# A decoder layer on one core: rotating the last block's k on GpSimd between the loops, and a last-stage softmax with one exponential

## The reference, cut to what matters

```python
q = (query @ Wq).reshape(nb, q_len, H, D).transpose(0, 2, 1, 3)
k = (key @ Wk).reshape(nb, q_len, KVH, D).transpose(0, 2, 1, 3)
...
q = q * cos + _rotate_half(q) * sin
k = k * cos + _rotate_half(k) * sin
...
scores = jnp.einsum('bhqd,bhkd->bhqk', q, k) / jnp.sqrt(jnp.float32(D))
scores = jnp.where(mask == 0, jnp.float32(-1000000000.0), scores)
attn = jax.nn.softmax(scores, axis=-1)
x = jnp.einsum('bhqk,bhkd->bhqd', attn, v)
return x.transpose(0, 2, 1, 3).reshape(nb, q_len, H * D) @ Wo
```

## Time and profile before

| | |
|---|---|
| median of 3 runs | 2348.61 us (2341.81 to 2349.77) |
| profiled execution | 2350.73 us |
| its span, first to last instruction | 2349.1 us |
| mean granted TensorE clock | 0.95 of full speed |
| busy: TensorE, VectorE | 2086.0 us (89%), 1762.5 us (75%) |
| busy: ScalarE, GpSimd | 1003.9 us (43%), 701.3 us (30%) |

### The profile page before, as it was taken

How to read it: one execution, slowest core, us unless ns; L and a number is a source line. 1 busy time by engine, 2 the same in 40 slices (tenths; PEclk the granted TensorE clock), 3 DMA queues, 4 the chain that set the end, 5 groups by cost and what they waited for, 6 DMA issues and landing times.

```text
span 2349.1 us, 26708 instructions
## 1 busy us (share of the span) xinstructions
PE 2086.0 (89%) x8268; PEld 1192.0 (51%) x8272; DVE 1762.5 (75%) x1735; ACT 1003.9 (43%) x2549; POOL 701.3 (30%) x492
## 2 busy tenths in 40 slices
PE   6877887898999988998999989998999989799988
PEld 2333454345555543445556544345556544477774
DVE  4499994459999996259999996259999994456553
ACT  2544440265555532155545541255545540233331
POOL 0289992401111112401111111501111110456550
PEclk9788999889999999989999999989999999799999
DMA  2579895527888873435888874525887874332210
GB/s 63 165 178 230 210 215 169 146 95 175 176 182 196 184 180 101 154 117 135 186 190 179 186 166 119 186 91 136 190 190 181 188 166 117 103 99 90 86 59 18
DMA packets 117810, 352.12 MB, mean 150 GB/s; under 512 B 14016, under 2 KB 14144, under 8 KB 115296
## 3 DMA queue, kind: packets, MB, share of 16 engines
q0 software_dynamic: 40704, 146.82, 32.3%
q1 hardware_dynamic: 70112, 191.68, 26.6%
q10 hardware_dynamic: 6912, 12.59, 1.4%
HBM read 197.68 MB, written 23.33 MB: 94 GB/s over the span
## 4 chain that ended last, share of the span: by engine, by line
DVE 34%; PE 27%; DMA 17%; issue 14%; ACT 3%; POOL 2%; DVEq 1%; PEldq 1%; SPq 0%; POOLq 0%; PEld 0%; ACTq 0%
DMA xc<-hs 15%; DVE hs L1254 11%; DVE hs L1431 4%; PE acc L1753 4%; PE acc L1631 3%; DVE hs L1261 3%; DVE hs L1245 2%; PE pq L1684 2%; PE acc L1837 2%; PE pq L1714 2%; PE pq L1921 2%; PE pk L1921 2%; PE acc L1766 1%; DVE pzsc L1311 1%; DVE qr L1291 1%
## 5 line engine op out<-in xcount | busy, mean ns | idle before, releaser
L768 POOL DMA_DIRECT2D xc<-hs x192 | 164.1, 860 | 1116.3 <-DVE hs L1261 1095.9
L1254 DVE TENSOR_TENSOR_SCAN hs<-dA,hs 128x1024 f32<-128x1024 f32 x192 | 428.7, 2274 | 0.0
L988 ACT ACTIVATE dA<-dt,aneg 128x504 f32<-128x504 f32 x384 | 253.6, 707 | 320.0 <-DVE hs L1254 319.8
L1684 PE MATMUL pq<-qT,wa 128*128 128x512 f32 x768 | 354.1, 615 | 15.1 <-DVE pzsc L1311 14.9
L1766 PE MATMUL acc<-wb,oT 128*128 128x512 f32 x768 | 352.2, 603 | 3.6 <-ACT oT L976 3.6
L1261 DVE TENSOR_TENSOR hs<-hs,bc 128x1024 f32<-128x1024 f32 x256 | 307.6, 1203 | 2.2
L953 ACT ACTIVATE pr<-pzsc,mx 128x64 f32<-128x64 f32 x512 | 170.8, 335 | 245.1 <-DVE mx L1317 245.1
L1245 DVE TENSOR_TENSOR hs<-u,bc 128x1024 f32<-128x1024 f32 x192 | 227.5, 1217 | 26.6 <-DMA xc<-hs 21.0
L1631 PE MATMUL acc<-xnT,wa 128*128 128x512 f32 x512 | 234.4, 612 | 14.3 <-DMA wa<-in_wx 3.9
L1684 PEld LDWEIGHTS pq<-qT,wa 128*128 128x128 f32 x768 | 146.4, 196 | 189.3 <-issue 177.2
L1766 PEld LDWEIGHTS acc<-wb,oT 128*128 128x128 f32 x768 | 141.2, 193 | 148.0 <-issue 143.9
(11 more groups left out here) (255 smaller groups left out, 3379.2 us busy)
## 6 DMA issues: line engine op xcount, KB each, us to landing
xc<-hs POOLq DMA_DIRECT2D x240, 512.0 KB, 7.0
bc<-bc_rows SPq DMA_DIRECT2D x64, 512.0 KB, 7.5
wa<-in_wq SPq DMA_DIRECT2D x64, 512.0 KB, 10.2
wb<-in_wo SPq DMA_DIRECT2D x64, 512.0 KB, 7.0
wa<-in_wx SPq DMA_DIRECT2D x16, 512.0 KB, 7.0
wa<-in_wz SPq DMA_DIRECT2D x16, 512.0 KB, 3.8
wb<-in_ow SPq DMA_DIRECT2D x16, 512.0 KB, 6.3
wv<-in_wv SPq DMA_DIRECT2D x26, 256.0 KB, 13.1
```

Source lines behind the costliest of these rows:

```text
L768: G.dma_start(xc[:, 2 * c:2 * c + 2, :], hs[:, c, :].rearrange("p (d t) -> p d t", t=T), accum_op=ALU.add).then_inc(s_y[c], 16)
L988: ins = S.activation(to[:, :, 1:SEQ], dt[:, s, :].rearrange("p (b t) -> p b t", t=SEQ)[:, :, 1:SEQ], ACT.Exp, scale=aneg[:, s, bass.ds(jj ...
L1254: V.tensor_tensor_scan(out=hs[:, c, :], data0=dA[:, c % 2, :], data1=hs[:, c, :], initial=0.0, op0=ALU.mult, op1=ALU.add).then_inc(scd.sem, 1)
L1684: ins = M.matmul(pq[:, h, :], wa4(p)[:, k, h * P:(h + 1) * P], qT[:, k, :], start=(k == 0), stop=(k == KE - 1))
```

## The change

Three things. GpSimd rotates the k of block 3 in the gaps after iterations 1 and 2, four heads (two pairs, m = 4 and 5) in each, with the cosines and sines of block 3, which SyncE loads into `oT`. Prefill, VectorE and SyncE wait for the larger counts. The last stage loads turned k straight into `kT`, and the load waits for the scores that read the head before. In the last stage VectorE adds the negated maximum to the scores, ScalarE takes one exponential of 512 columns, VectorE sums it; the high part of o is copied ahead of the exponential, and the low part is made between the sum with the maximum and the sum of the exponentials. The router's small buffers move to `kr` and `k1` for all blocks. The pieces below are in the order of the file: SyncE, GpSimd, ScalarE, VectorE.

```diff
-                            if p == 0 and mamba:
+                            if p == 0:
                                 eng.wait_ge(sd.sem, sd.upto(blk, 1) + jj * 2)
                                 hold(eng)
-                                load_turned_k(blk, jj + 1)
-                            elif p == 0:
-                                eng.wait_ge(krdy.sem, krdy.upto(0, 0) + jj)
-                                hold(eng)
-                                load_raw_k(blk, jj + 1)
+                                load_turned_k(blk, jj + 1, mamba)
...
                     if not nxt:
-                        load_raw_k(i, 0)
+                        eng.wait_ge(sd.sem, sd.upto(blk, PAIRS - 1))
+                        load_turned_k(i, 0, False)
...
+                if attn and nxt:
+                    eng.wait_ge(wod.sem, wod.upto(blk, PAIRS - 1))
+                    hold(eng)
+                    for c in range(2):
+                        eng.dma_start(oT[:, c, :], tscr[NBLK - 1, c]).then_inc(s_cs3, 16)
...
                     for n in range(2):
-                        eng.wait_ge(s_kst[n], i * 32 + 32)
+                        eng.wait_ge(s_kst[n], i * 48 + 32)
...
+                def heads_of(rows, m):
+
+                    if m < pairs:
+                        return rows[i, 2 * m:2 * m + 2]
+                    return rows[NBLK - 1, bass.ds((i - 1) * (KVH // 2) + 2 * (m - pairs), 2)]
...
-                def turn_pair(m):
+                def turn_pair(m, count):
 
                     raw, swp = turning[m % 2]
+                    cos, sin = (cosT[:, :], sinT[:, :]) if m < pairs else (oT[:, 0, :], oT[:, 1, :])
...
-                    if 1 <= m < KVH // 2 - 1:
+                    if 1 <= m < count - 1:
                         load_pair(m + 1)
...
-                    for m in range(KVH // 2):
-                        turn_pair(m)
+                    count = pairs + (2 if attn else 0)
+                    for m in range(count):
+                        if m == pairs:
+                            eng.wait_ge(s_cs3, i * 32)
+                            hold(eng)
+                        turn_pair(m, count)
...
                     if mamba:
-                        eng.wait_ge(s_kst[1], blk * 32 + 32)
+                        eng.wait_ge(s_kst[1], i * 48 - 16)
...
                     eng.wait_ge(smx.sem, smx.upto(blk, o) + jj * 2)
+                    if not mamba:
+                        S.activation(pr[:, :, :], pr[:, :, :], ACT.Exp).then_inc(exd.sem, 1)
+                        return
...
+                    if not mamba:
+                        evac_o(jj, p)
                     if attn and not last:
                         exps(jj, p + 1)
                     if mamba and not last:
                         decay(jj, p + 1, 0)
-                    if attn:
+                    if mamba and attn:
                         evac_o(jj, p)
...
+                def shift_scores(jj, o):
+
+                    eng.wait_ge(lmx.sem, lmx.upto(0, o) + jj * 2)
+                    V.tensor_tensor(pr[:, :, :], sc[:, :, :], mx[:, :].unsqueeze(2).to_broadcast([P, NB, SEQ]),
+                                    ALU.add).then_inc(smx.sem, 1)
+
+                def sum_probs(jj, o):
+
+                    eng.wait_ge(exd.sem, exd.upto(blk, o) + jj * 2)
+                    V.tensor_reduce(sm[:, :], pr[:, :, :], AX.X, ALU.add).then_inc(psm.sem, 1)
...
+                if mamba and attn:
+                    for n in range(2):
+                        eng.wait_ge(s_kst[n], i * 48 - 16)
...
-                    if not mamba and not tail and p == 0:
-                        rope_k(jj + 1)
...
+                    if soft and not mamba:
+                        shift_scores(jj, p + 1)
+                    if not mamba:
+                        o_low(jj, p)
+                    if soft and not mamba:
+                        sum_probs(jj, p + 1)
                     if soft:
                         invert_sum(jj, p + 1)
...
-                    if not mamba:
-                        o_low(jj, p)
```

More of the change, by code:

```diff
@@ L97, in build @@
         vscr = nc.dram_tensor("v_rows", (KVH, P, T), F32, kind="Internal").ap()
-        turned = nc.dram_tensor("k_turned_rows", (NBLK - 1, KVH, P, T), F32, kind="Internal").ap()
+        turned = nc.dram_tensor("k_turned_rows", (NBLK, KVH, P, T), F32, kind="Internal").ap()
         tscr = nc.dram_tensor("rotary_rows", (NBLK, 2, P, T), F32, kind="Internal").ap()
@@ L265, in build @@
         s_cs = sem("rotary_tables_loaded")
+        s_cs3 = sem("last_rotary_tables_loaded")
         s_kraw = [sem(f"raw_k_loaded{n}") for n in range(2)]
@@ L325, in build @@
         s_pid = sem("pos_index_ready")
-        kc1 = stage("pool_k_times_cos", KVH // 2)
-        kc2 = stage("pool_k_times_sin", KVH // 2)
-        kcd = stage("pool_k_turned", KVH // 2)
+        kc1 = stage("pool_k_times_cos", 6)
+        kc2 = stage("pool_k_times_sin", 6)
+        kcd = stage("pool_k_turned", 6)
         otd = stage("tail_o_done", TT)
@@ L334, in build @@
         qt2 = stage("q_times_sin", PAIRS)
-        kt1 = stage("k_times_cos", KVH)
-        kt2 = stage("k_times_sin", KVH)
         qrdy = stage("q_ready", PAIRS)
@@ L339, in build @@
         q2r = stage("q_sin_ready", PAIRS)
-        krdy = stage("k_ready", KVH)
         vrdy = stage("v_ready", KVH)
@@ L360, in build @@
         olo = stage("o_lo_ready", PAIRS)
+        lmx = stage("last_scores_max", PAIRS)
+        psm = stage("last_probs_summed", PAIRS)
         x2r = stage("x2_ready", TT)
@@ L536, in one, with load_turned_k @@
                 z_uses = W_DT if mamba else 0
-                def load_k(b, g, src, to, swapped):
-                    eng.dma_start(to[:, :], src[b, g]).then_inc(s_k1, 16)
-                    for h in range(2):
-                        eng.dma_start(swapped[h * 64:(h + 1) * 64, :], src[b, g, (1 - h) * 64:(2 - h) * 64, :]).then_inc(
+                def load_turned_k(b, g, halves=True):
+                    eng.dma_start(kT[:, :], turned[b, g]).then_inc(s_k1, 16)
+                    for h in range(2 if halves else 0):
+                        eng.dma_start(k2T[h * 64:(h + 1) * 64, :], turned[b, g, (1 - h) * 64:(2 - h) * 64, :]).then_inc(
                             s_kr, 16)
-                def load_raw_k(b, g):
-                    load_k(b, g, kscr, k1, kr)
-                def load_turned_k(b, g):
-                    load_k(b, g, turned, kT, k2T)
                 def load_tables(b):
@@ L837, in one, with turns, slot_use @@
                         rstd(i, ln2, ln2r, TT)
+                pairs = KVH // 2
+                def heads_of(rows, m):
+                    if m < pairs:
+                        return rows[i, 2 * m:2 * m + 2]
+                    return rows[NBLK - 1, bass.ds((i - 1) * (KVH // 2) + 2 * (m - pairs), 2)]
+                def turns(m):
+                    return (i * 6 - 2 if attn else 0) + (m + 1 + LEAD)
+                def slot_use(m):
+                    return (i * 3 - 1 if attn else 0) + m // 2
                 def load_pair(m):
@@ L1316, in max_scores @@
                     eng.wait_ge(srd.sem, srd.upto(blk, o) + jj * 2)
-                    V.tensor_reduce(mx[:, :], sc[:, :, :], AX.X, ALU.max, negate=True).then_inc(smx.sem, 1)
+                    V.tensor_reduce(mx[:, :], sc[:, :, :], AX.X, ALU.max, negate=True).then_inc(
+                        smx.sem if mamba else lmx.sem, 1)
+                def shift_scores(jj, o):
[5 more added lines that the diff above has]
+                    V.tensor_reduce(sm[:, :], pr[:, :, :], AX.X, ALU.add).then_inc(psm.sem, 1)
                 def invert_sum(jj, o):
-                    eng.wait_ge(exd.sem, exd.upto(blk, o) + jj * 2)
+                    if mamba:
+                        eng.wait_ge(exd.sem, exd.upto(blk, o) + jj * 2)
+                    else:
+                        eng.wait_ge(psm.sem, psm.upto(0, o) + jj * 2)
                     V.reciprocal(sm[:, :], sm[:, :]).then_inc(rcp.sem, 1)
@@ L1359, in one @@
                     eng.wait_ge(s_cs, blk * 32 + 32)
+                    rope_q(0, 0)
+                    mask_scores(0, 0)
+                    max_scores(0, 0)
                     if not mamba:
-                        rope_k(0)
-                    rope_q(0, 0)
-                    for part in (mask_scores, max_scores, invert_sum, probs):
-                        part(0, 0)
+                        shift_scores(0, 0)
+                        sum_probs(0, 0)
+                    invert_sum(0, 0)
+                    probs(0, 0)
                     rope_q(0, 1)
```

61 lines of the change are left out of this document (27 added, 34 removed).

## The result

In one comparison on the same chip the kernel before took 2345.58 us (median of 4 runs) and the changed one 2372.56 us (4 runs, 2368.15 to 2379.81): 27.0 us more, a ratio of 1.0118, 95% interval 1.0084 to 1.0151. That is slower, as forecast, and inside the range, but 13 us under the forecast of 2386. The profiled execution took 2374.11 us.

A forecast was written before the change was run, and what follows sets the result against it. The prefill's wait for GpSimd's k stores bounds the gaps, VectorE and SyncE's queue spoil the last stage: 2350.7 + 34.3 + 2.5 + 1 = 2388.5, with the median 2.1 lower 2386 us, range 2362 to 2398.

The forecast's parts named there:

- The bound of the gaps: Gaps 2 and 3: the prefill waits for GpSimd's k stores and holds the square; 34.3 us after 18.5 of room.
- 13.2, or 26.4 us a gap: Gaps 2 and 3: GpSimd's store-to-store interval for each new pair, two pairs a gap, 52.8 us for both gaps.
- The slower TensorE: Gaps 2 and 3, square to last scaling of xc: TensorE starts slower after the wait; half of 5.0, 2.5 us.
- The last stage: Rotation removed and softmax changed in the last stage: +1 us in sum, bounds -23 and +10.
- the walk: Last stage, followed from the mask: steps of 15.5 and 16.8 us, 32.3 against 31.8 before, six times, +3 us.
- The sign named for it: Last stage: wo splits of odd steps start 5 us after the mask, and two steps take 32 us.
- forecast -2: Start of the last stage: q's sine product of 3.20 us loses its blocker, 2 us less.
- The second spoiler: SyncE's queue, last stage: k's load waits for the scores, wo's behind it; wo split moves from -1.8 to +5.1.
- TensorE bounds: Last stage: wo lands early enough, or blocks fall between VectorE's instructions; 14.4 us a step, 2362 us; chance 0.17.
- The port: Last stage: VectorE's two-input SBUF work stands still beside GpSimd's difference, but only 0.89 us beside a one-input split.
- the second rival: Last stage: every split holds VectorE's two-input work for its whole length; 11 us more, 2397 us; chance 0.10.
- It lands within 8 us ... covered: Gaps: SyncE's output store, held until the last k is stored, lands before ScalarE overwrites dt; costs nothing.

The follow-up runs named there:

- rot_only: The changed kernel with the old softmax (eight exponentials, low part of o behind the scaling) back in the last stage: 2367.46 us, ratio 1.0097 to the kernel before.
- sp_order: The changed kernel with SyncE issuing the next wo load ahead of the scores' wait and the k load in the last stage: 2355.67 us, ratio 1.0056.
- no_diff: The changed kernel with GpSimd's two-input difference of each split replaced by a second one-input operation: 2358.41 us, ratio 1.0064 to the kernel before.
- before_sp: The kernel before with the next wo load issued ahead of the wait for rotated k and the k loads in the last stage: 2343.36 us, ratio 0.9998.
- sm_only: The kernel before with only the new softmax of the last stage, k still rotated there by VectorE: 2353.68 us, ratio 1.0043.
- before_act: The kernel before with the prefill moved behind ScalarE's copies of dt and VectorE itself waiting for the k stores: 2334.97 us, ratio 0.9962.

## Why the prediction was right, and where it was off

**The bound of the gaps: right.** The prefill, and the square behind it, were what turned GpSimd's work into time: moved, they give the time back. The first sign named, a prefill released by a k store, came in both gaps. For gap 3 the square's delay can be read: qT's copies begin at 1520.98, and before they began at 1515.77 and the square came 9.23 us later; so it would have been at 1530.2 and came at 1547.04, 16.8 later against 19 forecast.

**The growth of a gap: over-sized.** The term "13.2, or 26.4 us a gap" was too large. GpSimd's last store came 23.9 us later in gap 2 (67.8 us after its first product instead of 43.9) and 23.0 in gap 3 (59.6 after the first store instead of 36.6): 46.9 instead of 52.8. I had said that the new pairs run when nothing else moves data, but then priced them just under the rows with a load, in which the DMA engines were busy for 0.83 and 0.73 of the time. In gap 2 they were busy for 0.48 of the interval of pair 4, which holds a load and takes 11.5 us, and for 0.20 of that of pair 5, which holds none and takes 9.8. The growth is 11.9 us a pair in gap 2 and 11.5 in gap 3, at and just under the lower bound of 11.9.

**The slower TensorE: under-sized.** From the square to the last scaling both gaps now take 72.1 and 72.0 us, just as the first. That is the full 5 in this execution, and not half of it. In rot_only, sp_order and no_diff, whose gaps are the same, the two stretches exceed those of before by 2.9, 3.6 and 3.0 us, so the half was not a bad guess. Together, for this execution: 46.9 - 18.5 + 4.9 = 33.3 us, against 36.8 forecast and 33.6 in the table of stretches.

**The last stage: +1 forecast, +1.6 measured,** and the walk held where nothing else disturbed it: 15.4 and 16.2 us in three pairs of steps (from scores to scores), against 15.5 and 16.8. In two pairs it was 18.3 and 17.9, with the clock at 0.91 and 0.81, slow passes of the matmuls for it (7.18 us for q at 2155.77) and a rotation blocked for 3.29. The sign named for it came nearly as told: in the step shown the mask starts at 2171.14 and the split of wo 4.0 us later, against 5.1. That the sum came out so close is partly luck. Cut at the masks, the stage is 2.8 us shorter up to the third mask (forecast -2, though not where it was put: the first mask comes no earlier than before), 2.3 longer over the next twelve steps (forecast +3, from pairs of steps that are shorter than walked and two that are some 4 us longer), and 2.1 longer behind them, which the forecast did not have. The 31.8 us taken for two steps of before were a fast pair: the six pairs there take 32.5 in the mean, three of them with a step of 18.1. The second spoiler, the queue of SyncE, was the stronger, and the forecast never gave it a price of its own: without it the stage loses 19.6 us. The rival "TensorE bounds" (14.4 a step, -23) is what sp_order runs at, with 14.9 and -18 against the kernel before. So it was rightly a rival, and the condition named for it, "wo lands early enough", rightly the one that decides.

**The port: right.** A difference of GpSimd holds VectorE off until it ends; no_diff takes it away and gains 9 us in the stage. The reading "only the first 0.89 us of that one block", taken from one instruction of 1.36 us, holds too. In the changed kernel the scaling at 2175.39 begins 0.25 us after a one-input split and loses 0.65, the product at 2181.05 begins 0.28 after one and loses 0.61, and the scaling at 2139.66 begins 0.61 after one (2139.05) and loses 0.27: each is held until 0.88 to 0.90 us after GpSimd's start. The sum at 2187.94 begins 1.14 us after one (2186.80) and takes its usual 0.69. The rule of the Trainium skill (SBUF — State Buffer, Who interferes with whom), that the loser fully blocks, holds here for GpSimd's two-input instruction and not for its one-input one, which holds VectorE for 0.89 of 2.77 us. So the second rival, at 2397, was rightly put aside.

**What was costed at nothing.** "It lands within 8 us ... covered" held for the output store as long as the square was late too. Once the square moved, that store was the next wait (7.97 us in gap 3). The table loads into oT cost nothing that can be seen.

**The rest of the 13 us.** The kernel before came out at 2345.6 instead of 2348.6 in the later comparison: 3.0 of it. The gaps are 3.2 to 3.5. What is left, some 7, lies in stretches that the change hardly touches. The first one, up to the last scaling of gap 1, was long in the profiled execution of before alone: 524.1 us, 3.4 over the changed kernel, where the other kernels with the same code there took 519.1 to 521.8. The loops are shorter by 2.0, 0.9 and 1.2 us in the mean of four kernels with six pairs (the changed one, rot_only, sp_order, no_diff) against three with four (before, before_sp, sm_only). Single kernels of one kind scatter by 0.4 to 3.5 us there, so only the first of the three is clear of it, and before_act, with four pairs and the prefill moved, has a first loop of 405.40 us, as short as with six. **Why is open**; no run was made for it.

## What to carry to other kernels

A wait that stands first in a queue holds up all that is behind it: before pricing work added behind such a wait, look whether the waiting instruction can stand later, on its own engine and on the DMA queue. When an edit replaces what a queued DMA waits for, list the DMAs behind it: here a load of wo that was never late became what GpSimd waits for, 85 us in all, and moved its splits under VectorE's rotation of q; all because k now goes straight into a buffer that is still read. Eight slow instructions can be the cover under which another engine does its work; making them one only moves that work onto the chain.

## What the runs showed of the hardware

A one-input GpSimd instruction (128x1024, 2.77 us) held a VectorE instruction with two inputs from SBUF only until 0.88 to 0.90 us after its own start: the loss was 0.84, 0.65, 0.61 and 0.27 us for a VectorE instruction that began 0.05, 0.25, 0.28 and 0.61 us behind it, and nothing for one that began 1.14 us behind. A GpSimd instruction that began while such a VectorE instruction ran was held up itself (2.85 to 3.42 us in no_diff). GpSimd's two-input difference (2.40 us) held VectorE until it ended: 3.29 us instead of 1.23, ending 1.08 us after the difference. VectorE's product with the cosines, which reads one input from PSUM, took 1.22 to 1.23 us beside either. The blocked time in a stage hardly changed with the order of one DMA queue (86.6 and 89.5 us over four groups), while the stage changed by 19.6 us.
